# Gating of a windowed-attention and mixture-of-experts kernel, batched between its two stages, with a third score bank

## The chip, the cores and the metric

One Trainium2 chip, all 8 cores. Each core runs the same program on its own 2048 tokens and exchanges nothing. The metric is the device time of the slowest core in microseconds. Engines: TensorE (PE; PEld for its weight loads), VectorE (DVE), ScalarE (ACT), GpSimd (POOL, which here only issues DMAs), SyncE (SP, DMAs). PSUM, the memory TensorE writes, holds eight banks of 128 partitions x 512 float32.

## What is computed

Sliding-window attention over windows of 128 tokens with 16 heads of 64, a residual and a layernorm, then eight experts, top 2 of 8, computed densely for every token and weighted, residual and layernorm:

```python
qkv = x @ w_qkv                       # x (2, 8192, 1024)
scores = einsum('bhnqe,bhnke->bhnqk', q * scale, k_ctx)   # 128 queries x 384 keys
attn = softmax(where(valid, scores, NEG))
x1 = layernorm(x + einsum('bhnqk,bhnke->bhnqe', attn, v_ctx))
gate_probs = softmax(einsum('bsd,de->bse', x1, Wg) + bg)
topk_probs, topk_idx = top_k(gate_probs, 2)
weights = onehot(topk_idx) * topk_probs / sum(topk_probs)
h = gelu(einsum('bsd,edf->bsef', x1, W1) + b1)            # 8 experts, 1024 -> 4096
y = einsum('bsef,efd->bsed', h, W2) + b2
out = layernorm(x1 + einsum('bsed,bse->bsd', y, weights))
```

## The kernel before

The program is a list of instructions per engine, written by helpers `MM` (TensorE, all recorded at line 151), `DV` (VectorE, followed by a drain unless `drain=False`), `AC` (ScalarE), `SY` and `GP` (DMA issues of SyncE and GpSimd). Each engine runs its list strictly as emitted. The `waits` are semaphore counts; a `Bank` carries what must be done before its PSUM area may be written again.

**Projection stage.** q, k and v of the core's 2048 tokens and of one window either side.

**Attention stage.** 16 windows in 8 pairs; a pair is a block of 32 steps (two windows x 16 heads, alternating), 256 steps in all. Step g of the loop at L675 emits, in this order:
- `st_nm_exp(g)`: VectorE takes the negated row maximum of the scores (L401), ScalarE the exponential with its row sum (L409). In the core's first and last window a mask is added first (L393).
- `plan_scores(g+2)`: the 64 x 128 x 384 score matmul into bank g mod 2 of `ps_sc`, when the exponential of step g has read it.
- `st_tr(g)`: three transposes (matmuls with the identity) of the probabilities into `ps_pt`, two banks.
- `st_recip(g-2)` (L469), `st_evpt(g-1)`: copy of the transposed probabilities, by VectorE (L437) for even g-1 and by ScalarE (L432) for odd, `st_av(g-1)`: three matmuls with v.
- up to three divisions of attention outputs (`plan_evac`, L479), and when a window is complete the residual sum (L494) and the statistics (`plan_tail_stats1` to `3`), of which the last writes `x1tmp`, the normalised chunk (L549). In a block these fall into steps 1 and 4 (L494) and 4 and 7 (L549).
- one piece of the pending work of earlier windows, from `gen_tail_mm_pieces(j)`, nine per chunk j of 128 tokens: p1 four transposes of `x1tmp` into `ps_tm`, p2 its cast into `x1T` (L579), p3 and p4 the second half (L597), p5 the gate logits (a bias product in float32 and eight products with `wg_b`), p6 their maximum (L615) and exponential (L618), p7 to p9 eight VectorE operations on 128 x 8 (L625 to L638): the two largest, renormalised, into `wgt`. Pieces start in step 4 of the next block, one a step: the first chunk of the pair has steps 4 to 12, the second 13 to 21. So 14 of 16 chunks are handled inside the loop, and the last two behind it, piece by piece.

**Between the stages** (L764 on), PSUM is divided anew into `ps_h` (two tiles of two banks) and `ps_y` (the same). Sixteen times VectorE casts a chunk of `wgt` (L768) and TensorE transposes it; two copies make `wT_b` (L775); then for each chunk `wT_b` times the bias `b2` gives the first value of `y_acc` (two matmuls, one copy L787).

**Expert stage**, 32 units (8 experts x 4 quarters of 1024 hidden columns). A unit is 16 groups of 16 matmuls into `ps_h`, each followed by a Gelu of ScalarE into `hpr` (L888), the DMA of the next W1 quarter (L893, from GpSimd, behind the last group), then 16 chunks of 16 matmuls into `ps_y`, each followed by a multiply-add of VectorE into `y_acc` (L911), and the next W2 load (L923). An **end stage** adds `x1T` back, normalises and stores.

Of the kernel before, what the change touches and what calls it, by code (L numbers as in the profile page):

```python
# [85 lines left out]
def build_nc(debug=False):  # L86
# [26 lines left out]
    def psum(stk, name, shape):  # L113
        return stk.enter_context(nc.psum_tensor(name, shape, F32))
# [31 lines left out]
    def stc(c):  # L146
        return stats[:, c:c + 1]
# [192 lines left out]
    ps_sc = [psum(stk_C, f"ps_sc{i}", [128, 384]) for i in range(2)]  # L340
    bk_sc = [Bank(t[:], c_init) for t in ps_sc]
    ps_tm = psum(stk_C, "ps_tm", [128, 512])
    bk_tm = Bank(ps_tm[:], c_init)
# [31 lines left out]
    def plan_scores(g):  # L375
        w, h = steps[g]
        bi = g % 2
        scb[g] = bi
        hp, hb = h // 2, (h % 2) * 64
        w_ = list(bk_sc[bi].rw())  # L380
        if g < 2:
            w_ += [(s_ac, qkv_ac_end)]
        sc_v[g] = MM(ps_sc[bi][:],
                     q_b[hb:hb + 64, hp, 128 * w:128 * (w + 1)],
                     k_b[hb:hb + 64, hp, 128 * w:128 * w + 384],
                     start=True, stop=True, waits=w_, inc=s_mm)
# [170 lines left out]
    def gen_tail_mm_pieces(j):  # L557
        tm = {}

        def p1():  # L560
            mm = None
            for q4 in range(4):
                w_ = [(s_dv, x1ap_v[j])]
                if q4 == 0:
                    w_ += bk_tm.rw()
                    if state["wtail"] is not None:
                        w_.append((s_dv, state["wtail"]))
                    if state["ug"] is not None:
                        w_.append((s_ac, state["ug"]))
                    if debug:  # L570
                        w_.append((s_w, p.val[s_w]))
                mm = MM(ps_tm[:, 128 * q4:128 * q4 + 128],
                        x1tmp[:, j % 2, 128 * q4:128 * (q4 + 1)], I_b[:],
                        start=(q4 == 0), stop=(q4 == 3), waits=w_,
                        inc=(s_mm if q4 == 3 else None))
            tm["mm1"] = mm

        def p2():
            tm["cast1"] = DV((lambda _j: lambda v: v.tensor_copy(  # L579
                out=x1T[:, 0:4, 128 * _j:128 * (_j + 1)], in_=ps_tm[:, 0:512]))(j),  # L580
                waits=[(s_mm, tm["mm1"])], inc=s_dv, drain=False)

        def p3():
            mm = None
            for q4 in range(4):
                w_ = [(s_dv, x1ap_v[j])]
                if q4 == 0:
                    w_.append((s_dv, tm["cast1"]))
                mm = MM(ps_tm[:, 128 * q4:128 * q4 + 128],
                        x1tmp[:, j % 2, 128 * (4 + q4):128 * (5 + q4)], I_b[:],  # L590
                        start=(q4 == 0), stop=(q4 == 3), waits=w_,
                        inc=(s_mm if q4 == 3 else None))
            tm["mm2"] = mm
            x1tmm_v[j] = mm

        def p4():
            tm["cast2"] = DV((lambda _j: lambda v: v.tensor_copy(  # L597
                out=x1T[:, 4:8, 128 * _j:128 * (_j + 1)], in_=ps_tm[:, 0:512]))(j),
                waits=[(s_mm, tm["mm2"])], inc=s_dv, drain=False)

        def p5():
            MM(ps_tm[:, 0:8], ones_f[:], bg_s[:], start=True, stop=False,
               waits=[(s_dv, tm["cast2"]), (s_x, v_bg), (s_dv, v_ones)])
            gmm = None
            for dc in range(8):
                gmm = MM(ps_tm[:, 0:8], x1T[:, dc, 128 * j:128 * (j + 1)], wg_b[:, dc, :],
                         start=False, stop=(dc == 7),
                         waits=[(s_w, g_wg)], inc=(s_mm if dc == 7 else None))
            tm["gmm"] = gmm

        def p6():
            ngw = [(s_mm, tm["gmm"])]
            if state["ug"] is not None:
                ngw.append((s_ac, state["ug"]))
            nmg = DV(lambda v: v.reduce_max(out=stc(C_NMG), in_=ps_tm[:, 0:8],  # L615
                                            axis=AX.X, negate=True),
                     waits=ngw, inc=s_dv, drain=False)
            state["ug"] = AC(lambda s: s.activation(out=U8, in_=ps_tm[:, 0:8],  # L618
                                                    func=AF.Exp, bias=stc(C_NMG)),
                             waits=[(s_dv, nmg)] + ([(s_x, state["dbg_u"])] if state["dbg_u"] is not None else []),  # L620
                             inc=s_ac)
            bk_tm.release = [(s_dv, nmg), (s_ac, state["ug"])]

        def p7():
            DV(lambda v: v.reduce_max(out=stc(C_M2G), in_=U8, axis=AX.X), waits=[(s_ac, state["ug"])])  # L625
            DV(lambda v: v.tensor_scalar(out=G8A, in0=U8, scalar1=stc(C_M2G), scalar2=None, op0=ALU.is_ge))
            DV(lambda v: v.scalar_tensor_tensor(out=G8B, in0=G8A, scalar=-1e30, in1=U8,
                                                op0=ALU.mult, op1=ALU.add))

        def p8():  # L630
            DV(lambda v: v.reduce_max(out=stc(C_M2G), in_=G8B, axis=AX.X))
            DV(lambda v: v.tensor_scalar(out=G8A, in0=U8, scalar1=stc(C_M2G), scalar2=None, op0=ALU.is_ge))

        def p9():
            DV(lambda v: v.scalar_tensor_tensor(out=G8B, in0=U8, scalar=1.0, in1=G8A,
                                                op0=ALU.mult, op1=ALU.mult, accum_out=stc(C_SSG)))
            DV(lambda v: v.reciprocal(out=stc(C_RIG), in_=stc(C_SSG)))
            state["wtail"] = DV((lambda _j: lambda v: v.tensor_scalar(  # L638
                out=wgt[:, _j, :], in0=G8B, scalar1=stc(C_RIG), scalar2=None, op0=ALU.mult))(j),
                inc=s_dv)  # L640
            if debug:
                state["dbg_u"] = SY((lambda _j: lambda e: e.dma_start(
                    out=d_u[128 * _j:128 * (_j + 1), :], in_=U8))(j),
                    waits=[(s_dv, state["wtail"])], inc=s_x)

        return [p1, p2, p3, p4, p5, p6, p7, p8, p9]

    def plan_tail_mm(j, bt=None):
        for pc in gen_tail_mm_pieces(j):
            pc()  # L650
# [21 lines left out]
    plan_scores(1)  # L672
    for g in range(NST):
        w, h = steps[g]
        st_nm_exp(g)  # L675
        if g + 2 < NST:
            plan_scores(g + 2)
# [36 lines left out]
        if pend_tmpiece:  # L714
            pend_tmpiece.pop(0)()
# [17 lines left out]
    while pend_tmpiece:  # L733
        pend_tmpiece.pop(0)()
    pend_tailmm += [NCH - 2, NCH - 1]
    while pend_tailmm:
        plan_tail_mm(pend_tailmm.pop(0))
# [25 lines left out]
    wtmm = None  # L763
    prev_cp = None  # L764
    for i in range(NCH):
        g = i // 8
        cw = alias_w + ([(s_mm, wtmm)] if wtmm is not None else [])
        cp = DV((lambda _i: lambda v: v.tensor_copy(out=wb8[:], in_=wgt[:, _i, :]))(i),  # L768
                waits=cw, inc=s_dv, drain=False)
        w_ = [(s_dv, cp)] + bk_y[g].rw()  # L770
        wtmm = MM(ps_y[g][0:NEXP, 128 * (i % 8):128 * (i % 8) + 128], wb8[:], I_b[:],
                  start=(i % 4 == 0), stop=(i % 4 == 3), waits=w_, inc=s_mm)
    wt_ev = None
    for g in range(2):
        wt_ev = DV((lambda _g: lambda v: v.tensor_copy(out=wT_b[:, 1024 * _g:1024 * (_g + 1)],  # L775
                                                       in_=ps_y[_g][0:NEXP, :]))(g),
                   waits=[(s_mm, wtmm)], inc=s_dv, drain=False)

    for i in range(NCH):
        pp = i % 2  # L780
        gend = None
        for dh in range(2):
            w_ = [(s_dv, wt_ev), (s_w, g_b2)] + (bk_y[pp].rw() if dh == 0 else [])
            gend = MM(ps_y[pp][:, 512 * dh:512 * (dh + 1)], wT_b[:, 128 * i:128 * (i + 1)],
                      b2_b[:, 512 * dh:512 * (dh + 1)],
                      start=True, stop=True, waits=w_, inc=(s_mm if dh == 1 else None))
        ev = DV((lambda _i, _pp: lambda v: v.tensor_copy(out=y_acc[:, _i, :], in_=ps_y[_pp][:]))(i, pp),  # L787
                waits=[(s_mm, gend)], inc=s_dv)
        bk_y[pp].release = [(s_dv, ev)]
# [77 lines left out]
    for u in range(NUNIT):  # L867
# [3 lines left out]
        for pr in range(2):  # L871
            for fc in range(8):
                bank = bk_h[(pr * 8 + fc) % 2]
                gend = None
                for tt in range(2):
                    tq5 = pr * 2 + tt
                    for dc in range(8):
                        w_ = [(s_w, wld["w1", u])]
                        if tt == 0 and dc == 0:
# [14 lines left out]
                              waits=[(s_mm, hend)], inc=s_w) if u + 1 < NUNIT else None  # L894
        yend = None
        for tq in range(NCH):
# [3 lines left out]
            for dh in range(2):  # L900
# [13 lines left out]
                waits=[(s_mm, gend)], inc=s_dv)  # L914
# [12 lines left out]
    if debug:  # L927
        for i in range(NCH):
# [3 lines left out]
               inc=s_x)  # L932
# [59 lines left out]
```

## Time and profile before

| | us |
|---|---|
| median of 2 runs | 4786.56 (4511.9 and 5061.23) |
| profiled execution, slowest core | 4511.33 |
| its span, core 4 (first to last instruction) | 4509.8 |
| spans of the 8 cores | 4495.0 to 4509.8 |
| busy in the span: TensorE / VectorE / ScalarE | 4110.6 / 1141.3 / 902.6 |
| projection stage | 0 to 329 |
| attention stage, first to last exponential | 334.5 to 837 |
| last two chunks, `wT_b`, first `y_acc` | 837 to 901 |
| expert stage | 901 to about 4384 |

A busy time is a sum over stages. TensorE's matmuls are pipelined and their ends modelled, so busy is not the same as at peak. A timeline row gives the start, the duration, engine, line, operation, output<-inputs and, in brackets, how long the engine stood before it and what it then waited for; rows marked x3 merge neighbours. PEclk, the granted clock, is 1.00 at 2.4 GHz and 0.50 at 1.2 GHz.

### The profile page before, as it was taken

Reading aid. Unit: us, or ns where it says so; the run is one execution under the profiler, and the core shown is the slowest. Engines: PE = TensorE matmul, PEld = TensorE weight load, DVE = VectorE, ACT = ScalarE, POOL = GpSimd, SP = SyncE. Lnnn points to the kernel's source line nnn. Section 1 sums busy time; section 2 is a strip of 40 time slices with the busy share of each in tenths; the row PEclk is TensorE's granted clock in tenths of the full one; section 3 lists DMA queues with packets and bytes.
Section 4 is the critical chain, followed back from the end, with each engine's and each line's share of the span. In section 5 each row is a group of like instructions: output and inputs, shape, how many; then the busy total and the mean of one; then the engine's idle time right before and its main releaser. Section 6 shows DMA issues by size and latency. Waiting matters only on the chain.

```text
span 4509.8 us, 48636 instructions; the slowest of 8 cores (4495.0 to 4509.8 us)
## 1 busy us (share of the span) xinstructions
PE 4110.6 (91%) x19776; PEld 1915.0 (42%) x19776; DVE 1141.3 (25%) x1978; ACT 902.6 (20%) x1415; POOL 76.9 (2%) x92
## 2 busy tenths in 40 slices
PE   5875555499999999999999999999999999999995
PEld 3333333244444444444444444444444444444442
DVE  1116767611111111111111111111111111111126
ACT  1224444211111111111111111111111111111111
POOL 0000000000000000000000000000000000000000
PEclk9885555599999999999999999999999999999997
DMA  6542000012222222222222222222222222222211
GB/s 110 107 86 50 20 20 20 1 19 38 41 43 42 42 40 38 38 38 38 38 38 38 38 38 38 38 38 38 38 38 38 38 38 38 39 42 42 42 24 75
DMA packets 97483, 187.26 MB, mean 42 GB/s; under 512 B 3426, under 2 KB 24290, under 8 KB 97258
## 3 DMA queue, kind: packets, MB, share of 16 engines
q0 software_dynamic: 89616, 157.36, 20.1%
q1 hardware_dynamic: 7650, 26.81, 1.7%
q8 instruction: 161, 2.64, 0.2%
q14 instruction: 56, 0.46, 0.0%
HBM read 333.12 MB, written 8.39 MB: 76 GB/s over the span
## 4 chain that ended last, share of the span: by engine, by line
PE 87%; DVE 6%; issue 3%; DMA 2%; ACT 1%; DVEq 1%; ACTq 0%; POOLq 0%; SPq 0%
PE ps_h L151 39%; PE ps_y L151 39%; PE ps_qk L151 4%; PE ps_sc L151 2%; PE ps_pt L151 2%; DMA W1g<-wqkv 1%; DVE stats L401 1%; ACT probs_u L409 1%; DVEq L157 1%; DVE attn_sb L479 1%; DMA W2g<-wqkv 0%; DVE xpre L494 0%; PE ps_tm L151 0%; DVE probsT L437 0%; DVE y_acc L787 0%
## 5 line engine op out<-in xcount | busy, mean ns | idle before, releaser
L151 PE MATMUL ps_y<-W2g,hpr 128*128 128x512 bf16 x8192 | 1781.5, 380 | 0.0
L151 PE MATMUL ps_h<-x1T,W1g 128*128 128x512 bf16 x8192 | 1775.7, 380 | 0.0
L911 DVE SCALAR_TENSOR_TENSOR y_acc<-ps_y,wgt,y_acc 128x1024 f32<-128x1024 f32 x512 | 657.3, 1284 | 2866.7 <-PE ps_y L151 2866.1
L151 PEld LDWEIGHTS ps_y<-W2g,hpr 128*128 128x128 bf16 x8192 | 802.4, 98 | 970.0 <-issue 8.9
L151 PEld LDWEIGHTS ps_h<-x1T,W1g 128*128 128x128 bf16 x8192 | 801.5, 98 | 969.5 <-issue 4.0
L888 ACT ACTIVATE hpr<-ps_h,b1T 128x1024 bf16<-128x1024 f32 x512 | 569.9, 1113 | 2907.4 <-PE ps_h L151 2907.4
L151 PE MATMUL ps_sc<-k_b,q_b 64*128 64x384 bf16 x256 | 122.7, 480 | 204.6 <-ACT probs_u L409 202.8
L409 ACT ACTIVATE probs_u<-ps_sc,stats 128x384 bf16<-128x384 f32 x256 | 149.1, 582 | 231.6 <-DVE stats L469 224.9
L151 PE MATMUL ps_qk<-xT_S,W1g 128*128 128x512 bf16 (+3 forms) x640 | 141.9, 392 | 39.4 <-DMA W1g<-wqkv 32.4
L401 DVE TENSOR_REDUCE stats<-ps_sc 128x1 f32<-128x384 f32 x256 | 139.7, 549 | 8.8 <-issue 2.7
L151 PE MATMUL ps_pt<-I_b,probs_u 128*128 128x128 bf16 x768 | 128.6, 306 | 1.2 <-ACT probs_u L409 1.2
L151 PEld LDWEIGHTS ps_sc<-k_b,q_b 64*128 64x128 bf16 x256 | 25.8, 101 | 237.7 <-issue 233.6
L151 PEld LDWEIGHTS ps_qk<-xT_S,W1g 128*128 128x128 bf16 x640 | 66.9, 110 | 113.5 <-issue 66.9
L151 PEld LDWEIGHTS ps_pt<-I_b,probs_u 128*128 128x128 bf16 x768 | 61.3, 125 | 85.8 <-issue 85.8
L437 DVE CAST probsT<-ps_pt 128x384 bf16<-128x384 f32 x128 | 71.0, 555 | 96.2 <-PE ps_pt L151 95.3
L151 PE MATMUL ps_av<-v_b,probsT 128*128 128x64 bf16 x768 | 94.1, 248 | 0.6 <-ACT probsT L432 0.6
L151 PEld LDWEIGHTS ps_av<-v_b,probsT 128*128 128x128 bf16 x768 | 76.6, 142 | 1.9 <-issue 0.9
L248 DVE CAST xT_S<-ps_tr 128x512 bf16<-128x512 f32 x18 | 12.5, 692 | 217.6 <-PE ps_tr L151 217.6
L893 POOL DMA_DIRECT2D W1g<-w x31 | 27.1, 874 | 2258.5 <-PE ps_h L151 2258.5
L151 PE MATMUL ps_qk<-W2g,xT_S 128*128 128x512 bf16 x288 | 63.7, 382 | 0.0
L479 DVE TENSOR_SCALAR attn_sb<-ps_av,stats 128x64 bf16<-128x64 f32 x256 | 57.3, 274 | 18.0 <-PE ps_av L151 17.8
L432 ACT CAST probsT<-ps_pt 128x384 bf16<-128x384 f32 x128 | 59.9, 468 | 0.9 <-PE ps_pt L151 0.9
(89 smaller groups left out, 674.7 us busy)
## 6 DMA issues: line engine op xcount, KB each, us to landing
W1g<-w POOLq DMA_DIRECT2D x32, 2048.0 KB, 14.2
W2g<-w POOLq DMA_DIRECT2D x32, 2048.0 KB, 13.2
W1g<-wqkv POOLq DMA_DIRECT2D x20, 1024.0 KB, 9.7
xch_q<-xh SPq DMA_DIRECT2D x18, 512.0 KB
xch<-xh SPq DMA_DIRECT2D x16, 512.0 KB
out<-outb SPq DMA_DIRECT2D x16, 512.0 KB, 2.6
W2g<-wqkv POOLq DMA_DIRECT2D x1, 2048.0 KB, 21.0
mask_s<-maskl SPq DMA_DIRECT2D x1, 192.0 KB
```

The costliest lines, as they stand in the source:

```text
L151: lambda t: t.matmul(_d, _l, _r, start=_s, stop=_e))(dst, lhsT, rhs, start, stop)
L157: p.op("vector", lambda v: v.drain())
L248: DV((lambda _jr, _bk, _sp: lambda v: v.tensor_copy(out=xT_S[:, _sp, 0:4, _jr:_jr + 128], in_=_bk.ap[:, 0:512]))(jr, bank, sp), waits=evw, ...
L401: nmv = DV((lambda _bi, _bp: lambda v: v.reduce_max(out=stc(C_NM + _bp), in_=ps_sc[_bi][:], axis=AX.X, negate=True))(bi, bp), waits=nmw, i ...
L409: exp_v[g] = AC((lambda _bi, _bp, _s: lambda s: s.activation(out=probs_u[:, _bp, :], in_=ps_sc[_bi][:], func=AF.Exp, bias=stc(C_NM + _bp), ...
L432: ev = AC((lambda _b, _s: lambda s: s.copy(out=probsT[:, _s, :], in_=ps_pt[_b][:, 0:384]))(bt, sl), waits=epw, inc=s_ac)
L437: ev = DV((lambda _b, _s: lambda v: v.tensor_copy(out=probsT[:, _s, :], in_=ps_pt[_b][:, 0:384]))(bt, sl), waits=epw, inc=s_dv, drain=False)
L479: evac_v[(w, h)] = DV((lambda _w, _h, _aw, _s: lambda v: v.tensor_scalar(out=attn_sb[:, _w % 2, 64 * _h:64 * _h + 64], in0=ps_av[_aw][:, 6 ...
L888: gel_pr[pr] = AC((lambda _fc, _pr, _bk, _col: lambda s: s.activation(out=hpr[:, _fc, 1024 * _pr:1024 * (_pr + 1)], in_=_bk.ap[:], func=AF ...
L893: wld["w1", u + 1] = GP((lambda _u: lambda e_: e_.dma_start(out=W1g[:], in_=w1_ap(_u)))(u + 1), waits=[(s_mm, hend)], inc=s_w) if u + 1 < ...
L911: ev = DV((lambda _tq, _pp, _e: lambda v: v.scalar_tensor_tensor(out=y_acc[:, _tq, :], in0=ps_y[_pp][:], scalar=wgt[:, _tq, _e:_e + 1], in ...
```

## The change

Three edits in one. The score tiles get a third PSUM bank, taken from `ps_tm`, and scores are emitted three steps ahead. The transposes of `x1tmp` go into the bank of `ps_pt` that the step does not use, and each cast is emitted in the same step as its transposes: two pieces per chunk (`p12`, `p34`) instead of nine. The gate (logits, exponential, top 2) leaves the loop: it is made for all 16 chunks in one batch behind the attention stage, with all logits in one bank of `ps_y`, and two alternating sets of small tiles. The code that makes `wT_b` and the first `y_acc` is wrapped in `emit_wt_yinit` and called inside unit 0, behind its hidden groups.

```diff
-    ps_sc = [psum(stk_C, f"ps_sc{i}", [128, 384]) for i in range(2)]
+    ps_sc = [psum(stk_C, f"ps_sc{i}", [128, 384]) for i in range(3)]
     bk_sc = [Bank(t[:], c_init) for t in ps_sc]
-    ps_tm = psum(stk_C, "ps_tm", [128, 512])
-    bk_tm = Bank(ps_tm[:], c_init)
...
-        bi = g % 2
+        bi = g % 3
...
+        def p12(bank):
             mm = None
             for q4 in range(4):
                 w_ = [(s_dv, x1ap_v[j])]
                 if q4 == 0:
+                    w_ += bk_pt[bank].rw()
...
+                mm = MM(ps_pt[bank][:, 128 * q4:128 * q4 + 128],
                         x1tmp[:, j % 2, 128 * q4:128 * (q4 + 1)], I_b[:],
...
+            cast = DV((lambda _j, _b: lambda v: v.tensor_copy(
+                out=x1T[:, 0:4, 128 * _j:128 * (_j + 1)], in_=ps_pt[_b][:, 0:512]))(j, bank),
+                waits=[(s_mm, mm)], inc=s_dv, drain=False)
+            bk_pt[bank].release = [(s_dv, cast)]
...
+        return [p12, p34]
...
-        if g + 2 < NST:
-            plan_scores(g + 2)
+        if g + 3 < NST:
+            plan_scores(g + 3)
...
-            pend_tmpiece.pop(0)()
+            pend_tmpiece.pop(0)((g + 1) % 2)
...
+    for tq in range(NCH):
+        w_ = ([(s_dv, win_dv_end), (s_x, v_bg), (s_dv, v_ones)] + bk_y[0].rw()) if tq == 0 else []
+        MM(ps_y[0][:, 8 * tq:8 * tq + 8], ones_f[:], bg_s[:],
+           start=(tq == 0), stop=False, waits=w_)
+    glast = None
+    for tq in range(NCH):
+        for dc in range(8):
+            glast = MM(ps_y[0][:, 8 * tq:8 * tq + 8], x1T[:, dc, 128 * tq:128 * (tq + 1)],
+                       wg_b[:, dc, :], start=False, stop=(tq == NCH - 1 and dc == 7),
...
+    for tq in range(NCH):
+        par = tq % 2
+        U8p = U8s[par]
+        nmg = DV((lambda _t, _p: lambda v: v.reduce_max(out=stc(CGNM[_p]), in_=ps_y[0][:, 8 * _t:8 * _t + 8],
+                                                        axis=AX.X, negate=True))(tq, par),
+                 waits=[(s_mm, glast)], inc=s_dv, drain=False)
...
+        ug = AC((lambda _t, _p, _u: lambda s: s.activation(out=_u, in_=ps_y[0][:, 8 * _t:8 * _t + 8],
+                                                           func=AF.Exp, bias=stc(CGNM[_p])))(tq, par, U8p),
+                waits=ugw, inc=s_ac)
+        DV((lambda _p, _u: lambda v: v.reduce_max(out=stc(CGM2[_p]), in_=_u, axis=AX.X))(par, U8p),
+           waits=[(s_ac, ug)])
...
+        wtail_v[tq] = DV((lambda _t, _p: lambda v: v.tensor_scalar(
+            out=wgt[:, _t, :], in0=G8B, scalar1=stc(CGRI[_p]), scalar2=None, op0=ALU.mult))(tq, par),
+            inc=s_dv)
...
+    def emit_wt_yinit():
...
         wld["w1", u + 1] = GP((lambda _u: lambda e_: e_.dma_start(out=W1g[:], in_=w1_ap(_u)))(u + 1),
                               waits=[(s_mm, hend)], inc=s_w) if u + 1 < NUNIT else None
+        if u == 0:
+            emit_wt_yinit()
...
-                waits=[(s_mm, gend)], inc=s_dv)
+                waits=[(s_mm, gend), (s_dv, wtail_v[tq])], inc=s_dv)
```

Left out of the quoted diff: the rest of the VectorE operations on 128 x 8 (the same eight as in p7 to p9), the body of `emit_wt_yinit` (as before, with a wait for the chunk's `wgt`), and waits that only a debug build has.

## Rows read from the trace of the kernel before

**Rows 1.** Windows: stretch, length, busy us by engine, PEclk, DMA, GB/s.
```profile
334.50:836.90 502.40, 293.82 (x2030) 173.34 (x2031) 351.03 (x1187) 237.19 (x707) 0.00 (x0) 0.50 0.10 26
...
865.90:901.00 35.10, 20.13 (x49) 3.57 (x49) 23.16 (x33) 0.00 (x0) 0.00 (x0) 0.50 0.00 1
901.00:906.00 5.00, 5.00 (x13) 1.80 (x13) 1.52 (x2) 0.00 (x0) 0.00 (x0) 0.51 0.00 0
```

**Rows 2.** Waits of VectorE in the attention stage: total us, times, longest.
```profile
DVE probsT L437 <- PE ps_pt L151: 92.2, 98, 1.6
...
DVE stats L401 <- issue: 2.7, 14, 0.4
```

**Rows 3.** Timeline, ScalarE, block steps 5, 6, 8, 12, 16, 24, 30, 32.
```profile
408.36 0.58 ACT L409 ACTIVATE probs_u<-ps_sc,stats 128x384 bf16<-128x384 f32 x1 [0.94 <-DVE stats L469]
...
410.57 0.58 ACT L409 ACTIVATE probs_u<-ps_sc,stats 128x384 bf16<-128x384 f32 x1 [0.61 <-DVE stats L469]
...
415.38 0.58 ACT L409 ACTIVATE probs_u<-ps_sc,stats 128x384 bf16<-128x384 f32 x1 [3.19 <-DVE stats L469]
...
422.42 0.58 ACT L409 ACTIVATE probs_u<-ps_sc,stats 128x384 bf16<-128x384 f32 x1 [1.40 <-DVE stats L469]
...
430.71 0.58 ACT L409 ACTIVATE probs_u<-ps_sc,stats 128x384 bf16<-128x384 f32 x1 [2.55 <-DVE stats L469]
...
445.28 0.58 ACT L409 ACTIVATE probs_u<-ps_sc,stats 128x384 bf16<-128x384 f32 x1 [1.33 <-DVE stats L469]
...
454.12 0.58 ACT L409 ACTIVATE probs_u<-ps_sc,stats 128x384 bf16<-128x384 f32 x1 [1.34 <-DVE stats L469]
...
458.44 0.58 ACT L409 ACTIVATE probs_u<-ps_sc,stats 128x384 bf16<-128x384 f32 x1 [2.71 <-DVE stats L469]
```

**Rows 4.** Timeline of the same block, VectorE, ScalarE and TensorE.
```profile
426.24 0.69 DVE L579 CAST x1T<-ps_tm 128x512 bf16<-128x512 f32 x1 [0.90 <-PE ps_tm L151]
...
427.49 0.58 ACT L409 ACTIVATE probs_u<-ps_sc,stats 128x384 bf16<-128x384 f32 x1 [1.09 <-DVE stats L469]
...
429.19 0.61 PE L151 MATMUL ps_tm<-I_b,x1tmp 128*128 128x128 bf16 x4
...
430.60 0.65 DVE L479 TENSOR_SCALAR attn_sb<-ps_av,stats 128x64 bf16<-128x64 f32 x3
...
444.16 0.56 DVE L437 CAST probsT<-ps_pt 128x384 bf16<-128x384 f32 x1 [1.33 <-PE ps_pt L151]
```

**Rows 5.** Timeline behind the last attention step.
```profile
844.89 0.81 DVE L549 TENSOR_SCALAR x1tmp<-xpre,stats 128x1024 bf16<-128x1024 f32 x1
...
845.85 0.58 PE L151 MATMUL ps_tm<-I_b,x1tmp 128*128 128x128 bf16 x4 [6.62 <-DVE x1tmp L549]
...
852.89 0.69 DVE L579 CAST x1T<-ps_tm 128x512 bf16<-128x512 f32 x1 [0.16 <-issue]
...
862.10 0.50 PEld L151 LDWEIGHTS ps_tm<-bg_s,ones_f 1*128 1x128 f32 x2 [1.18 <-issue]
...
862.63 0.29 PEld L151 LDWEIGHTS ps_tm<-wg_b,x1T 128*128 128x128 bf16 x8
...
863.11 0.17 DVE L615 TENSOR_REDUCE stats<-ps_tm 128x1 f32<-128x8 f32 x1 [1.12 <-PE ps_tm L151]
863.37 0.27 ACT L618 ACTIVATE stats<-ps_tm,stats 128x8 f32<-128x8 f32 x1 [6.61 <-DVE stats L615]
...
865.56 0.23 DVE L638 TENSOR_SCALAR wgt<-stats 128x8 f32<-128x8 f32 x1
```

**Rows 6.** Timeline: the first `wT_b` product.
```profile
866.38 0.27 PE L151 MATMUL ps_y<-I_b,wb 128*8 128x128 bf16 x1 [3.38 <-DVE wb L768]
```

**Rows 7.** Timeline: ScalarE in the first unit, and its first W2 product.
```profile
907.11 1.28 ACT L888 ACT_TABLE_LOAD   x1 [43.47 <-PE ps_h L151]
...
917.49 1.11 ACT L888 ACTIVATE hpr<-ps_h,b1T 128x1024 bf16<-128x1024 f32 x1 [2.34 <-PE ps_h L151]
...
958.67 7.50 PE L151 MATMUL ps_y<-W2g,hpr 128*128 128x512 bf16 x34
```

## What the change does to the time: the prediction

> **What bounds the kernel now.** I read the windows table first, because the change touches three stages with different limits. In the attention stage (334.5 to 836.9) TensorE is busy 294 of 502 us at a granted clock of 0.50, VectorE 351 of 502: nobody is full, so a loop of latencies sets the pace, and saved work counts only where it lies on that loop. From 865.9 to 901.0 the kernel makes `wT_b` and the first `y_acc`: 35.1 us in which the expert matmuls have not begun. After 901 they run at full clock without gaps, so everything that delays them is paid in full [rows 1].
>
> Next the waits of VectorE inside the attention stage. Its costliest is the copy of the transposed probabilities (L437), 92.2 us behind TensorE; the row maximum (L401), the one reader of a score tile that comes first, never waits on the score matmuls: its largest entry is 2.7 us of "issue" [rows 2]. So scores are always early with two banks.
>
> Then the exponentials in order of time, one per step; their starts give each step's length. I number steps 0 to 31 in a block (one pair of windows). Plain pairs of steps take (454.12 - 445.28)/3 = 2.95 us; a pair with three divisions behind the attention output takes 458.44 - 454.12 = 4.32 [rows 3]. Inside a plain pair, L437 starts 1.12 us before the next even exponential (444.16 against 445.28), so 2.95 - 1.12 = 1.83 after the even one [rows 4]. The loop is: exponential, score matmul, transposes, L437 (1.83), then 1.12 to the next. VectorE work in an even step hides in the 1.33 that L437 waits; work in an odd step (behind L437) is paid.
>
> **Part 1, third score bank, scores three steps ahead.** TensorE still meets the score matmul at the same place of its queue, behind the same wait (the exponential of step g frees the bank), ahead of the same transposes. What moves is when a score is ready, and nobody waits for that [rows 2]. Cost 0, gain 0. The cover is one step of lead; it was enough before.
>
> **Part 2, gate work leaves the attention loop.** It goes from 14 of 16 chunks, two per block, in 7 blocks. By the exponentials of one block, before against what stays:
> - steps 10 and 11 become a plain pair, 2.95; what that gives is inside the sum for steps 8 to 11 in part 3.
> - steps 12 to 15 take 430.71 - 422.42 = 8.29; without the cast that sat in step 14 a plain pair and one with divisions remain: 2.95 + 4.32 = 7.27. Gain 1.02.
> - steps 16 to 23 take 445.28 - 430.71 = 14.57; without gate work, two pairs with three divisions whose input is ready (2.95 and the 0.65 of three divisions [rows 4]) and two plain ones: 13.10. Gain 1.47.
>
> **Part 3, the cast follows its transposes in the same step.** Before, a piece of TensorE work and the cast of it were a step apart. Now VectorE is sent to the cast at once, and everything queued behind it there (the next row maximum, hence the next exponential, hence scores and transposes) stands still.
> - Steps 4 and 7 (first half of a chunk, right behind `x1tmp`): matmuls start 0.15 after `x1tmp` ends (844.89 + 0.81 = 845.70 to 845.85) and last 0.58, so the cast starts 0.84 after it, where a cast without wait starts at 0.16 (the wait in the row of 852.89) [rows 5]. Step 7: +0.68. Step 4 had no cast: +0.68 and the cast's 0.69 = +1.37.
> - Steps 5 and 8 (second half): TensorE reaches the four matmuls 1.70 after the exponential (427.49 to 429.19), they last 0.61, 0.11 to the cast: 2.42. From a cast's start to the next exponential is 427.49 - 426.24 = 1.25. So such a step takes 3.67 [rows 4]. Step 5 took 410.57 - 408.36 = 2.21: +1.46. Steps 8 to 11 took 422.42 - 415.38 = 7.04 [rows 3]; now 3.67, then 1.12 (L437 waits no longer), then a plain pair 2.95: 7.74, +0.70.
>
> Block: 1.37 + 1.46 + 0.68 + 0.70 - 1.02 - 1.47 = +1.7; seven blocks **+12 us**. If the casts cost nothing new, steps 8 to 11 would be two plain pairs (-1.14) and the block would gain 1.14 + 1.02 + 1.47 = 3.6, seven 25 us; if the removed work gave nothing, it would lose 1.37 + 1.46 + 0.68 + (3.67 + 1.12 - 2.95) = 5.35, seven 37 us. Range of this part -25 to +37; I take +12, since each term has its row.
>
> **Part 4, gate as one batch ahead of the experts.** Casts from 852.89: 0.69, then the last chunk's transposes (0.12 + 0.59), 0.11, and two casts of 0.69: 855.8. Then 16 bias products of 0.50 and 16 times eight gate products of 0.29, with 0.19 (862.92 to 863.11) to the first reader: 16 x 0.79 + 0.2 = 12.8, so the first L615 stands at 868.7 [rows 5]. The batch is bounded by 4.6 (only gate products count) and by 16 x 1.01 = 16.
>
> Then sixteen chains. One is L615 to the end of L638: 865.79 - 863.11 = 2.68, and a gap between none and the 0.16 of the 852.89 row, for which I take 0.08: 2.76 (sixteen gaps make it uncertain by 1.3 us). VectorE does them in order, and each holds one ScalarE exponential that waits for its maximum. All sixteen stand in ScalarE's queue ahead of the first Gelu. The last starts 15 x 2.76 = 41.4 after the first maximum and ends 0.53 after its own (863.11 to 863.64) [rows 5]: 910.6. The Gelu table load 1.28 and the first Gelu 1.11 follow: 913.1 with the steps between [rows 7]. The `ps_h` banks are two: TensorE does two groups of 16 matmuls (from 868.5 on, hidden) and stands until 913.1. Fourteen groups remain at 1.11 + 2.34 = 3.45: 48.3 [rows 7].
>
> **Part 5, `wT_b` and `y_acc` move behind the first expert's hidden stage.** The piece is not overlapped by the move: its first matmul is in TensorE's queue behind all of the hidden stage, and the W2 products are behind it. From 866.38 [rows 6] to 901.0 [rows 1] is 34.6; its pace is set by VectorE copies, so I keep 34.6. The W1 load behind it on the gpsimd queue waits only for the hidden stage; it has the whole second stage as before.
>
> Clock: the one start that the trace shows, 901.0 to 906.0, ran at 0.51 granted and 1.00 after [rows 1], so it cost half of 5 us. TensorE was lightly used before it (20 of 35 us). Now there are two such starts on the path, at 913.1 and after `y_acc`: 2 x 2.5, where before one. The Trainium skill ("TensorE: Matmul & The Clock Gate", section HAM oscillation) says that a kernel whose TensorE stops between bursts pays the slow start at each burst. By the trace's single start alone 5 us less would be paid; by the rule the 5 stand.
>
> Sum of parts 4 and 5: 913.1 + 48.3 + 2.5 + 34.6 + 2.5 = 1001.0, against the first W2 product at 958.67 [rows 7] (its own slow start is in it): **+42 us**, bounds +34 (batch at 4.6) and +46. Afterwards nothing differs: 31 units and the end stage are the same.
>
> Total: 4511.3 + 12 + 42 = **4565 us**. The profiled execution (4511.33) agrees with the lower of the two runs (4511.9); the median given, 4786.56, is the mean of that run and one of 5061.23, and the sum isn't made against it.
>
> **Rivals.**
> (a) The gate chain hides under the hidden stage. This is so if ScalarE could do Gelu between the sixteen exponentials. Then hidden work starts at 868.5 instead of 901.0, ends at 926.2, and 34.6 + 2.5 gives 963.3: +5, in all 4511 + 12 + 5 = 4528. Against it: one ScalarE queue, in program order, as the rows of L618 and L888 show it everywhere else.
> (b) The casts don't hold VectorE up (transposes done earlier than I think): 4511 + 42 - 25 = 4528. Against it: L579 waited 0.90 for its matmuls even a step later [rows 4].
> (c) Faster: the third bank breaks the latency loop and the stage runs at VectorE's busy time. VectorE's whole idle time there is 502 - 351 = 151 us [rows 1], so 4565 - 151 = 4414, -2.2%. It decides only if nearly all idle goes; with the waits of rows 2 alone (92) it is 4473. Against it: the loop runs through exponential and transposes, not through scores.
> (d) Slower by over 2%: the clock stays at 0.50 for the whole hidden stage behind the stall. Fourteen groups at twice 3.45 cost 48 more instead of 2.5: 4565 + 46 = 4611, +2.2%; it decides from about 12 slow groups of 14. Against it: 5 us sufficed at 901.
> (e) Both (a) and (b): 4511 + 5 - 25 = 4491, no slower than before; it has both reasons against it.
>
> **How the numbers follow.** Forecast (within about 30 us of 4565) 0.70; (a) 0.08; (b) 0.10; (c) 0.02; (d) 0.08; (e) 0.02. The predicted time is the forecast's. Range 4525 to 4593: from (a) and (b), with 3 us for their own error, to +37 with +46 (4594) nearly; it leaves out (c), (d), (e) and the corners where all bounds meet. The range of the forecast alone is 4535 to 4593. Two per cent, about what a measurement of this kernel tells from no change, is 90 us: 4421 to 4602. Faster 0.02 is (c); slower 0.09 is (d) and a batch worse than its bound; within 0.89.
>
> **What would show it.** In the profile after: the Gelu table load near 910 (plus the attention stage's shift), directly behind sixteen exponentials 2.76 apart, and a TensorE gap of about 35 us between the second and third group; W2 products 42 us later than the attention stage's own shift explains; the casts that follow L579 and L597 each waiting 0.7 to 2 us for the transposes; blocks 1.7 us longer; L437's waits little changed in plain pairs. Wrong if plain pairs become shorter than 2.95 (the third bank matters), if Gelu 0 comes before the last gate exponential, or if the granted clock after the stall stays at 0.50.

## The result

The changed kernel takes 4560.27 us (median of 11 runs) against 4521.22 (median of 10 of the kernel before); the ratio is 1.0115, 95% interval 1.0081 to 1.0149. So it is slower by 1.15%, some 52 us, and the whole interval lies above 1. The medians hold some executions in which the cores of a die took longer at a lower granted clock; the ratio leaves these out, and the profiles below are read on cores that were not slowed.

The forecast time was 4565, the range 4525 to 4593: both held. What failed is the reading of it: the prediction called this "within 2%" with a chance of 0.89, as if that were no change; the last bullets of the section on the prediction come back to it.

The profile after, on core 4 (span 4552.8; before, the same core has 4509.8). The windows table, columns as in [rows 1]:

```profile
334.50:839.30 504.80, 280.31 (x1877) 160.47 (x1878) 325.18 (x1041) 230.92 (x689) 0.00 (x0) 0.50 0.10 24
...
868.80:878.50 9.70, 9.70 (x38) 3.68 (x35) 5.34 (x32) 1.07 (x4) 0.00 (x0) 0.72 0.00 1
878.50:914.60 36.10, 0.10 (x2) 0.10 (x2) 21.82 (x130) 5.83 (x15) 0.00 (x0) 0.53 0.00 0
914.60:918.70 4.10, 4.10 (x11) 1.39 (x12) 0.00 (x0) 0.79 (x1) 0.00 (x0) 0.52 0.00 0
918.70:965.30 46.60, 46.47 (x216) 20.88 (x214) 0.00 (x0) 14.68 (x14) 0.00 (x0) 1.00 0.00 1
965.30:1003.20 37.90, 22.79 (x55) 4.69 (x56) 24.54 (x33) 0.93 (x1) 0.87 (x1) 0.56 0.32 56
```

The attention stage lasts 508.9 us from the first to the last exponential (330.7 to 839.6), against 502.4. The third row is new: 36.1 us in which TensorE does nothing, between the second and third group of the expert stage. The granted clock is 0.52 for the 4.1 us behind it and then 1.00; at 901 in [rows 1] it was 0.51 for 5 us.

The timeline from the gate batch to the first W2 results:

```profile
858.47 6.96 PE L151 MATMUL ps_y<-bg_s,ones_f 1*128 1x8 f32 x32 [1.05 <-DVE x1T L586]
...
865.37 3.58 PE L151 MATMUL ps_y<-wg_b,x1T 128*128 128x8 bf16 x128
...
869.05 0.17 DVE L732 TENSOR_REDUCE stats<-ps_y 128x1 f32<-128x8 f32 x1 [10.83 <-PE ps_y L151]
...
871.86 0.17 DVE L732 TENSOR_REDUCE stats<-ps_y 128x1 f32<-128x8 f32 x1
...
911.98 1.28 ACT L888 ACT_TABLE_LOAD   x1
...
913.27 2.12 ACT L888 ACTIVATE hpr<-ps_h,b1T 128x1024 bf16<-128x1024 f32 x2
...
914.53 7.75 PE L151 MATMUL ps_h<-x1T,W1g 128*128 128x512 bf16 x26 [36.01 <-ACT hpr L888]
...
964.95 0.22 PE L151 MATMUL ps_y<-I_b,wb 128*8 128x128 bf16 x1
...
1000.04 20.18 PE L151 MATMUL ps_y<-W2g,hpr 128*128 128x512 bf16 x84 [0.38 <-DVE y_acc L787]
...
1005.66 1.28 DVE L913 SCALAR_TENSOR_TENSOR y_acc<-ps_y,wgt,y_acc 128x1024 f32<-128x1024 f32 x1 [4.39 <-PE ps_y L151]
```

The bias and gate products take 10.6 us (858.47 to 869.05); the maxima L732 follow each other by 2.8; the Gelu's table load starts at 911.98, when the sixteenth exponential is done; TensorE goes on at 914.53, having waited 36.0 us on ScalarE's Gelu (36.01 in its row). `wT_b` and `y_acc` run from 964.95 to 1000.04, W2 from there. From the last exponential of attention to the first multiply-add (L913) it is 1005.66 - 839.6 = 166.1 us. Before, by VectorE's row

```profile
962.40 1.28 DVE L911 SCALAR_TENSOR_TENSOR y_acc<-ps_y,wgt,y_acc 128x1024 f32<-128x1024 f32 x1 [59.72 <-PE ps_y L151]
```

it was 962.40 - 836.9 = 125.5: +40.6. With +6.4 of the attention stage that is +47; the attention stage of this core happened to begin 3.7 us earlier (330.7 against 334.5), which gives the 43.0 by which the spans differ.

The steps of one block, answering [rows 3] (exponentials of steps 5, 6, 8 and 12, ScalarE timeline):

```profile
405.54 0.58 ACT L407 ACTIVATE probs_u<-ps_sc,stats 128x384 bf16<-128x384 f32 x1 [2.21 <-DVE stats L467]
...
409.20 0.58 ACT L407 ACTIVATE probs_u<-ps_sc,stats 128x384 bf16<-128x384 f32 x1 [2.06 <-DVE stats L467]
...
414.69 0.58 ACT L407 ACTIVATE probs_u<-ps_sc,stats 128x384 bf16<-128x384 f32 x1 [3.87 <-DVE stats L467]
...
422.33 0.58 ACT L407 ACTIVATE probs_u<-ps_sc,stats 128x384 bf16<-128x384 f32 x1 [1.10 <-DVE stats L467]
```

and the two casts of the first chunk in it, VectorE timeline:

```profile
404.29 0.69 DVE L570 CAST x1T<-ps_pt 128x512 bf16<-128x512 f32 x1 [0.83 <-PE ps_pt L151]
...
407.95 0.69 DVE L586 CAST x1T<-ps_pt 128x512 bf16<-128x512 f32 x1 [1.41 <-PE ps_pt L151]
```

Step 5 takes 3.66 us (before 2.21), steps 8 to 11 take 7.64 (before 7.04). The casts waited 0.83 and 1.41 for transposes of the same step. VectorE's waits over the stage, answering [rows 2]:

```profile
DVE probsT L435 <- PE ps_pt L151: 114.8, 105, 1.6
DVE x1T L586 <- PE ps_pt L151: 26.9, 14, 2.4
DVE x1T L570 <- PE ps_pt L151: 11.7, 14, 0.8
```

The same view of the kernel before has

```profile
DVE x1T L579 <- PE ps_tm L151: 6.9, 7, 1.5
...
DVE x1T L597 <- PE ps_av L151: 1.5, 7, 0.5
```

so the casts waited 8.4 us in all, and now their successors wait 38.6.

### The profile page after: what moved, and what is told of

Its sections match the earlier page's. It is cut to its first block, busy times and chain, and to the rows that moved or that the text cites. A ratio compares the mean times of both kernels' runs of the same rounds, so it can differ in the third digit from the quotient of the medians.

```text
span 4556.2 us, 48557 instructions; the slowest of 8 cores (4541.9 to 4556.2 us)
## 1 busy us (share of the span) xinstructions
PE 4107.2 (90%) x19776; PEld 1912.0 (42%) x19776; DVE 1141.6 (25%) x1978; ACT 902.3 (20%) x1415; POOL 76.6 (2%) x92
## 4 chain that ended last, share of the span: by engine, by line
PE 86%; DVE 6%; issue 3%; DMA 2%; ACT 1%; DVEq 1%; ACTq 0%; POOLq 0%; SPq 0%
PE ps_y L151 39%; PE ps_h L151 39%; PE ps_qk L151 4%; PE ps_pt L151 2%; DVE stats L399 2%; PE ps_sc L151 2%; DMA W1g<-wqkv 2%; ACT probs_u L407 1%; DVEq L157 1%; DVE attn_sb L477 1%; DMA W2g<-wqkv 0%; DVE xpre L492 0%; DVE y_acc L787 0%; DVE outb L855 0%; DVE probsT L435 0%
## 5 line engine op out<-in xcount | busy, mean ns | idle before, releaser
L151 PE MATMUL ps_h<-x1T,W1g 128*128 128x512 bf16 x8192 | 1778.0, 380 | 36.1 <-ACT hpr L888 36.1
L913 DVE SCALAR_TENSOR_TENSOR y_acc<-ps_y,wgt,y_acc 128x1024 f32<-128x1024 f32 x512 | 657.3, 1284 | 2811.3 <-PE ps_y L151 2810.7
L435 DVE CAST probsT<-ps_pt 128x384 bf16<-128x384 f32 x128 | 71.1, 556 | 121.4 <-PE ps_pt L151 118.9
```

What stands on the lines that cost most here:

```text
L151: lambda t: t.matmul(_d, _l, _r, start=_s, stop=_e))(dst, lhsT, rhs, start, stop)
L435: ev = DV((lambda _b, _s: lambda v: v.tensor_copy(out=probsT[:, _s, :], in_=ps_pt[_b][:, 0:384]))(bt, sl), waits=epw, inc=s_dv, drain=False)
L913: ev = DV((lambda _tq, _pp, _e: lambda v: v.scalar_tensor_tensor(out=y_acc[:, _tq, :], in0=ps_y[_pp][:], scalar=wgt[:, _tq, _e:_e + 1], in ...
```

## The experiments

The question for each: which of the edits costs, and by which mechanism. My theory is the one of the prediction: the third bank does nothing, casts and gate removal together cost a few us, the sixteen chains ahead of the first Gelu in ScalarE's queue are the bulk, and `y_acc` costs the same at either place. Rivals are named with each run.

**1. Two score banks.**

```diff
-    ps_sc = [psum(stk_C, f"ps_sc{i}", [128, 384]) for i in range(3)]
+    ps_sc = [psum(stk_C, f"ps_sc{i}", [128, 384]) for i in range(2)]
-        if g + 3 < NST:
-            plan_scores(g + 3)
+        if g + 2 < NST:
+            plan_scores(g + 2)
```

> The changed kernel with the old number of score banks (two) and scores two steps ahead; nothing else differs. Theory: the third bank buys nothing, because no reader of a score tile waited for the score matmul before; the ratio to the kernel before stays at that of the changed kernel, 1.0115, within 0.001 (5 us), and blocks of 32 steps stay at 63.9 to 64.0 us. Rival: the third bank gives a gain that the casts in the same step eat up; then blocks grow by 1 us or more and the time by 10 us or more.

Measured: ratio 1.0118 (1.0083 to 1.0152); attention stage 508.6 against 508.9, the block of the rows above 63.95 in both. With two banks VectorE waits 3.2 us in all for scores (2.6 before the row maximum, 0.6 before the mask), with three not at all, but the stage doesn't get longer by it. So the third bank changes no time that can be seen, and it didn't hide a loss either.

**2. A tile of its own for the transposes of `x1tmp`, each cast a step behind them.**

```diff
-    ps_sc = [psum(stk_C, f"ps_sc{i}", [128, 384]) for i in range(3)]
+    ps_sc = [psum(stk_C, f"ps_sc{i}", [128, 384]) for i in range(2)]
+    ps_tm = psum(stk_C, "ps_tm", [128, 512])
+    bk_tm = Bank(ps_tm[:], c_init)
...
-        return [p12, p34]
+        return [pm(0), pc(0), pm(1), pc(1)]
```

(`pm` emits four transposes into `ps_tm`, `pc` the cast; scores two steps ahead as in run 1.)

> The changed kernel with the transposes of x1tmp in a tile of their own and each cast one step after its transposes (four pieces, two score banks); the gate stays in its batch. Theory: VectorE no longer stands before the casts (38.6 us in the changed kernel). By the step sums steps 4 and 5 fall from 8.69 to 5.97, steps 6 and 7 from 5.49 to 4.81, steps 8 to 11 become two plain pairs with a cast of 0.69 each, 7.28 after 7.64: 3.8 us a block, seven blocks 26 us, so 4534 us, ratio about 1.006; blocks of 60.2 us. Rival (the bank of the transposes and the cast's place cost nothing, the attention stage is longer for another reason): no change from 4560.

Its first executions give no ratio, so the same kernel was run again:

> The same kernel as own_tile, for its time: the attention stage was 482.1 us (first to last exponential) against 509.0 of the changed kernel and 502.4 of the one before, and the last two chunks cost 2.7 more behind it. Theory: 24 us less than the changed kernel, 4536, ratio 1.006. Rival (what the stage gains is given back later): 4560.

Measured: ratio 1.0073 (1.0047 to 1.0099), where the changed kernel has 1.0115; the attention stage lasts 482.1 us, 27 less than with the casts in the same step and 20 less than before the change. The first exponentials of two successive blocks (ScalarE timeline, core 0) and VectorE's waits there:

```profile
385.84 0.58 ACT L409 ACTIVATE probs_u<-ps_sc,stats 128x384 bf16<-128x384 f32 x1 [2.70 <-DVE stats L469]
...
446.19 0.58 ACT L409 ACTIVATE probs_u<-ps_sc,stats 128x384 bf16<-128x384 f32 x1 [2.70 <-DVE stats L469]
```

```profile
DVE probsT L437 <- PE ps_pt L151: 120.7, 105, 1.6
...
DVE x1T L579 <- PE ps_av L151: 1.1, 7, 0.2
...
DVE x1T L579 <- PE ps_sc L151: 0.4, 1, 0.4
```

A block takes 60.35, against 63.95 in the changed kernel and 62.68 before: 3.6 less than in the changed kernel where 3.8 was expected. The casts' waits are all but gone (1.5 us is left), while L437 waits 120.7 us instead of 114.8: L437's wait is not what has to be shortened, it is where the latency loop shows. So two opposed effects were in the attention stage. This kernel's attention loop is that of the kernel before without the gate work, so taking the gate out is worth 20 us; the casts as the change places them cost 27. Run 1 is the control that this isn't the number of score banks. The run takes away two things together, the cast in the same step and the bank shared with `ps_pt`. What speaks for the first is that the casts' own waits fall from 38.6 to 1.5 us, and that in the changed kernel's attention stage no wait of TensorE ends with a cast of `x1T`; the shared bank alone was not run. Of the gain 2.5 us is returned behind the stage (169.6 from the last exponential to the first multiply-add on core 0, 167.1 in the changed kernel on the same core), where the last two chunks now go through one tile.

**3. `wT_b` and first `y_acc` ahead of the hidden stage, as before the change.**

```diff
+    emit_wt_yinit()
+
     tbank = [bk_h[0], bk_y[0]]
...
-        if u == 0:
-            emit_wt_yinit()
```

> The changed kernel with wT_b and the first y_acc made ahead of the hidden stage, as before the change; the gate batch stays. Theory: the 34.6 us are on the path at either place; here the two hidden groups (9.7 us) no longer lie under the gate chains, but the table load (1.3), the first Gelu (1.1) and one slow start (2.3) fall away: 5 us slower than the changed kernel, 4565. Rival (moving that piece behind the hidden stage is what costs, by its restart of the clock and its place beside the W1 load): faster than the changed kernel by 5 to 35 us.

Measured: ratio 1.0110 (1.0066 to 1.0153); from the last exponential to the first multiply-add 171.0 us against 166.1 (core 4): +4.9. TensorE's timeline shows why nothing is won:

```profile
858.02 3.57 PE L151 MATMUL ps_y<-wg_b,x1T 128*128 128x8 bf16 x128
907.36 0.27 PE L151 MATMUL ps_y<-I_b,wb 128*8 128x128 bf16 x1 [45.77 <-DVE wb L768]
...
942.73 56.95 PE L151 MATMUL ps_h<-x1T,W1g 128*128 128x512 bf16 x250 [0.33 <-issue]
999.52 6.64 PE L151 MATMUL ps_y<-W2g,hpr 128*128 128x512 bf16 x30
```

TensorE waits 45.8 us for the chains ahead of `wT_b` instead of 36.0 behind two hidden groups. The hidden stage starts only at 942.73, runs without a gap and ends at 999.5. The expected 5 us are there in the stage; in the total they are below what the interval tells. The rival (the move costs) falls: moving the piece back doesn't bring back any of the 40.6.

**4. One gate chain behind each of the first sixteen Gelus.**

```diff
-    for tq in range(NCH):
+    def gate_chain(tq):
         par = tq % 2
...
                 bank.release = [(s_ac, gel_pr[pr])]
+                if u == 0:
+                    gate_chain(pr * 8 + fc)
```

> The changed kernel with one gate chain emitted behind each of the first unit's sixteen Gelus instead of sixteen ahead of the first; same operations. Theory (order of ScalarE's queue): TensorE's gap of 36.0 us before the third group closes, and the hidden stage starts full behind 868.8. But Exp and Gelu alternate; if each change loads a table of 1.28, a group costs ScalarE 1.11 + 1.28 + 0.27 + 1.28 = 3.94 instead of the 3.45 of TensorE, 8 us over sixteen groups: 4560 - 36 - 2 + 8 = 4530. Rival 1 (the clock is the cost, the gap is there for another reason): 4555 or more. Rival 2 (no table loads between): 4522.

Measured: ratio 1.0044 (1.0020 to 1.0067), some 32 us below the changed kernel by the ratios, whose intervals are 10 and 15 us to each side. The trace is sharper: the last exponential to the first multiply-add takes 143.5 us, 22.6 less, with the attention stage the same (508.8). ScalarE's timeline between two Gelus:

```profile
919.60 1.28 ACT L737 ACT_TABLE_LOAD   x1
920.90 0.27 ACT L737 ACTIVATE stats<-ps_y,stats 128x8 f32<-128x8 f32 x1
921.18 1.28 ACT L887 ACT_TABLE_LOAD   x1
922.48 1.11 ACT L887 ACTIVATE hpr<-ps_h,b1T 128x1024 bf16<-128x1024 f32 x1
923.65 1.28 ACT L737 ACT_TABLE_LOAD   x1
```

Same operations, another order in the queues, and TensorE's gap of 36.0 us is gone (0.4 to 0.8 us is left before most groups): the order is the cause of it. The row pattern also shows what this order costs: a table load of 1.28 us before the exponential and one before the Gelu, so that a group takes 4.05 (919.60 to 923.65) where TensorE needs 3.45. Rival 2 (no loads) falls, and rival 1 with it. The expectation of 30 us less missed one wait, which TensorE's timeline has behind the hidden stage:

```profile
936.12 0.26 PE L151 MATMUL ps_y<-I_b,wb 128*8 128x128 bf16 x1 [8.77 <-DVE wb L767]
```

`wT_b` now waits 8.8 us for the end of the last chains, which come with the last Gelus.

**5. One chain over all chunks.**

```diff
-    nmg = ug = None
-    for tq in range(NCH):
...
+    DV(lambda v: v.reduce_max(out=g_m[:], in_=L3, axis=AX.X), waits=alias_w + [(s_mm, glast)])
+    sbv = DV(lambda v: v.tensor_tensor(out=g_u[:], in0=L3, in1=bc(g_m), op=ALU.subtract), inc=s_dv)
+    ug = AC(lambda s: s.activation(out=g_u[:], in_=g_u[:], func=AF.Exp), waits=[(s_dv, sbv)], inc=s_ac)
+    DV(lambda v: v.reduce_max(out=g_m[:], in_=g_u[:], axis=AX.X), waits=[(s_ac, ug)])
+    DV(lambda v: v.tensor_tensor(out=g_a[:], in0=g_u[:], in1=bc(g_m), op=ALU.is_ge))
...
```

> The changed kernel with the sixteen gate chains replaced by one chain over all sixteen chunks (tiles of 128 x 16 x 8): the same steps, eleven VectorE operations and one ScalarE exponential. Theory: the gap of 36.0 us before the third hidden group is the length of the chains ahead of the first Gelu; with a chain of about 4 us it is gone, together with the slow start behind it (2.3): 39 us less than the changed kernel, 4521, ratio 1.003. What stays over the kernel before is the longer attention stage (+6.4). Rival (the restart of the clock or the move of the first y_acc holds the time): 4550 or more.

Measured: ratio 1.0017 (1.0002 to 1.0032), 44 us below the changed kernel by the ratios and 39.1 by the stage behind the attention. VectorE's first and last operation of the chain, then ScalarE, then TensorE:

```profile
861.16 0.29 DVE L737 TENSOR_REDUCE g_m<-ps_y 128x16 f32<-128x128 f32 x1 [10.84 <-PE ps_y L151]
...
865.21 0.29 DVE L748 TENSOR_TENSOR wgt<-g_b,g_m 128x128 f32<-128x128 f32 x1
```

```profile
866.35 1.28 ACT L878 ACT_TABLE_LOAD   x1 [4.12 <-PE ps_h L151]
867.64 1.11 ACT L878 ACTIVATE hpr<-ps_h,b1T 128x1024 bf16<-128x1024 f32 x1
869.82 1.11 ACT L878 ACTIVATE hpr<-ps_h,b1T 128x1024 bf16<-128x1024 f32 x1 [1.06 <-PE ps_h L151]
```

```profile
861.29 23.97 PE L151 MATMUL ps_h<-x1T,W1g 128*128 128x512 bf16 x101 [0.24 <-issue]
```

The chain takes 4.3 us (861.16 to 865.50) where sixteen took 45, because an operation on 128 x 128 takes 0.28 or 0.29 us where one on 128 x 8 takes 0.16 to 0.23: the time was in the count, not in the elements. The table load waits only for the first group, TensorE has no gap, and the last exponential to the first multiply-add is 127.0 us (125.5 before). What stays is the attention stage (508.8). That closes the account: 39.1 of the 40.6 us behind the attention stage were the chains ahead of the first Gelu, with the slow start that followed TensorE's stop.

**6. Own tile, one chain, and `wT_b` and `y_acc` between the hidden groups.**

```diff
                 bank.release = [(s_ac, gel_pr[pr])]
+                if u == 0:
+                    gi = pr * 8 + fc
+                    if gi == 1:
+                        wt_part()
+                    if 3 <= gi <= 10:
+                        yinit(2 * (gi - 3))
+                        yinit(2 * (gi - 3) + 1)
```

(`wt_part` makes `wT_b`, with one cast of all of `wgt` instead of sixteen that alternate with the transposes; `yinit` makes the first `y_acc` of one chunk. The own tile and the one chain are as in runs 2 and 5.)

> own_tile with the single gate chain, and with wT_b and the first y_acc laid between the hidden groups of the first unit (transposes behind group 1, two chunks of y_acc behind each of groups 3 to 10). Theory, by stages: attention 482.1; last exponential to the first hidden product 32; hidden stage 57.7 plus 9 us of TensorE's own work for wT_b and y_acc; first multiply-add 3.7 later: 102 us from the last exponential, where the kernel before needs 125.5. With the attention stage 43 us less than before: 4469, ratio 0.990. Rival (TensorE stands for the VectorE copies of 1.23 each as in the piece of 34.6 us): ratio 0.996 or more.

Measured: ratio 0.9905 (0.9888 to 0.9923), median 4470.12: faster than both kernels. By stages the attention takes 482.1 us, and the last exponential to the first multiply-add 102.9 (102 expected). TensorE:

```profile
837.37 8.85 PE L151 MATMUL ps_h<-x1T,W1g 128*128 128x512 bf16 x31 [0.24 <-issue]
846.15 1.06 PE L151 MATMUL ps_y<-I_b,wb_all 128*8 128x128 bf16 x16
...
854.15 1.03 PE L151 MATMUL ps_y<-b_b,wT_b 8*128 8x512 bf16 x4
855.12 3.63 PE L151 MATMUL ps_h<-x1T,W1g 128*128 128x512 bf16 x16
...
904.27 21.10 PE L151 MATMUL ps_y<-W2g,hpr 128*128 128x512 bf16 x96
```

Between two groups lie 1.0 us of products for two chunks of `y_acc`, and no wait for the copies of VectorE, which run under the next group. So the piece of 34.6 us of [rows 6] has become 9.2 us: the hidden stage takes 66.9 us (837.37 to 904.27) with it, and took 57.7 without it (901.0 to 958.67 before). The rival falls. W2 starts 99.3 us behind the last exponential (804.94), where the kernel before needs 121.8.

## Why the prediction was right and where it failed

- **Third bank, 0.** Right: run 1. The stage doesn't change, though with two banks the changed kernel has 3.2 us of small waits for scores.
- **Gate work out of the loop, casts at once.** Right in mechanism, and close in size for the block that was worked out: steps 4 and 5 +2.72 (forecast +2.83), 6 and 7 +0.68 (+0.68), 8 to 11 +0.60 (+0.70), 12 to 15 -1.09 (-1.02), 16 to 23 -1.64 (-1.47), together +1.27 for +1.7. The mis-sized term is "seven blocks +12 us": it measured +6.4. Six of the blocks got 0.6 to 1.9 us longer, 1.2 on the mean, which makes 2.9 of the missing 5.4 us; the block with the core's last window, where every second step has a mask, got 0.5 shorter (2.2 of the 5.4), and the first block, which has no gate work, 0.4 shorter. I had multiplied one block by seven without looking whether the last one was like it.
- **Batch ahead of the experts.** 12.8 us forecast, 10.6 measured: sixteen bias products in a row took 0.43 each (6.96 for 32 records, two a product), not the 0.50 of one alone, and eight gate products 0.22 (3.58 for 128), not 0.29; each accounts for one us. Chains: 2.76 apart forecast, 2.8 measured; first maximum to table load 41.9 against 42.9. The gap of 36.0 us was forecast as about 35, and runs 4 and 5 show that it comes from the order in ScalarE's queue and from the length of the chains.
- **`y_acc` at the new place, 34.6 each way.** 35.1 measured (964.95 to 1000.04).
- **Two slow starts instead of one.** Right in kind, and each a little smaller than the 2.5 forecast. The first ran at 0.52 for 4.1 us, and fourteen groups took 50.4 us (914.53 to 964.95) where 48.3 were reckoned at full clock: 2.1. Behind `y_acc` it is 5.62 us from the first W2 product to the first multiply-add where it was 3.73: 1.9 more than before, where the trace had granted 1.00 by then. The trace agrees with the rule cited from the Trainium skill ("TensorE: Matmul & The Clock Gate", section HAM oscillation) in that both breaks are followed by a slow start. Only the first is a stop; in the second TensorE was busy with short products, with no wait longer than 2.6 us. Parts 4 and 5 together: +42 forecast, +40.6 measured.
- **Total.** +54 forecast, +47 by the stages of one core, +52 by the ratio (37 to 67 by its interval).
- **What failed**, beside the size of the attention term, is the step from the sum to the chances: "Two per cent, about what a measurement of this kernel tells from no change, is 90 us". The measured ratio has an interval of 0.34% to each side, 15 us, and run 5 is told from no change at 0.17% with 0.15% to each side. A sum of +54 us, with a range of its own from +24 to +82, said "slower" on every path of the forecast and of (d); (a) and (b), at +17, lie just outside such an interval, and only (c) and (e) were below zero. So "within 0.89" put the forecast's own +54 us down as no change, and slower got 0.09. I had no row for the 2%. The profiled execution of 4511.33 next to the run of 4511.9 was the one hint, and it pointed to much less than that. By the prediction's own chances for its paths (0.70, and 0.08, 0.10 and 0.08 for (a), (b) and (d)), slower should have had 0.9 or more.
- **Rivals.** (a) is false of the edit as made: the table load comes behind the sixteenth exponential. The order that it supposes was tried in run 4 and gives 22.6 us where (a) had 37, because each change between exponential and Gelu loads a table and the last chains hold `wT_b` back. (b) falls with the 38.6 us of waits, and (e), which needs both, with them. (c) falls: plain pairs still take 2.95, L435 waits longer than L437 did before, and run 1 shows no effect. (d) falls: 0.52 for 4.1 us, then 1.00.

## What to carry to other kernels

A batch of small work laid "under" a dense stage hides only if no engine of that stage has the batch ahead of its first piece in program order: sixteen short exponentials ahead of one Gelu stopped TensorE for 36 us. Spreading the batch over the stage has its own price if two functions then alternate on ScalarE (two table loads of 1.28 us a group in run 4). When many small operations in series are moved, look first whether they can be one: 4.3 us instead of 45. And in a loop paced by latency, a consumer emitted right behind its producer stalls everything queued behind it; one step of distance, with a bank of its own, was worth 27 us here, more than the 20 us of the work that was taken out of the loop.

## What the runs showed of the chip that I had not expected

- VectorE's cost of a small operation hardly grows with its elements: in float32 it took 0.16 to 0.23 us on 128 x 8, and 0.28 or 0.29 on 128 x 128, sixteen times the elements.
- Float32 bias products with one row took 0.22 us per record (two records a product) back to back against 0.25 in the pair alone.
- The granted clock fell although TensorE went on working: from 978 to 1000 it was busy 16.0 of 22.0 us with the short products of `y_acc`, at 0.50 granted, where the hidden stage before it had 1.00.
